# Recurrence steps threaded into the second output chunk, residual copies on two engines, and the second biases split earlier, in a two-layer kernel on one Trainium2 core

## The reference, cut to what matters

```
x = x + ffn0(cond0(x, cond))      # ffn0: gate/up products, quantised to 16 bits, sigmoid, down product
x = x + ffn1(cond1(x, cond))      # cond1: a recurrence over 128 steps; ffn1: 8 experts, top 2

cond1:  xw = x @ Wx + b
        h_t = tanh(xw_t + h_(t-1) @ Wh)          # 16 rows of 128, t = 0..127
ffn1:   logits = h @ router.T; top 2, softmax
        y = sum over the 2 of  gate * (gelu(h @ w1[e].T + b1[e]) @ w2[e].T + b2[e])
```

## Time and profile before

| | |
|---|---|
| Time, median of 3 runs | 302.99 us |
| Span of the profiled execution | 301.2 us |
| TensorE busy | 264.4 us, 88% |
| VectorE busy | 258.8 us, 86% |
| ScalarE busy | 215.6 us, 72% |
| GpSimd busy | 76.2 us, 25% |
| Mean granted TensorE clock | 0.947 |

### The profile page before, as it was taken

One profiled execution on the slowest core, in us unless ns is written; L12 is line 12 of the kernel. 1 busy time (PEld: TensorE's weight loads), 2 busy tenths in 40 slices (PEclk: granted clock), 3 DMA queues, 4 the chain that ended last, 5 costly groups with the idle time before them and its releaser, 6 DMA issues.

```text
span 301.2 us, 8834 instructions
## 1 busy us (share of the span) xinstructions
PE 264.4 (88%) x2716; PEld 205.5 (68%) x2716; DVE 258.8 (86%) x635; ACT 215.6 (72%) x455; POOL 76.2 (25%) x148
## 2 busy tenths in 40 slices
PE   4969940049989999999999999999999999999994
PEld 4824440016956777778888788888777887888874
DVE  4888999989898897779988799887799988889885
ACT  6367899998842677767777676667566766689892
POOL 3367997000025413011302112212110311101000
PEclk9989976557999999999999999999999999999999
DMA  6990443101500000000000000000001000001000
GB/s 186 314 310 4 84 94 76 28 0 35 90 17 2 0 3 1 0 2 2 19 0 0 2 3 26 2 0 0 1 2 30 8 0 0 2 1 37 0 2 27
DMA packets 24031, 10.63 MB, mean 35 GB/s; under 512 B 13355, under 2 KB 22982, under 8 KB 24006
## 3 DMA queue, kind: packets, MB, share of 16 engines
q1 hardware_dynamic: 23470, 10.05, 13.6%
q10 hardware_dynamic: 536, 0.26, 0.3%
HBM read 6.11 MB, written 1.05 MB: 24 GB/s over the span
## 4 chain that ended last, share of the span: by engine, by line
PE 79%; DVE 16%; issue 1%; ACT 1%; DMA 1%; SPq 0%; DVEq 0%
PE bank L893 78%; DVE peak L706 3%; DVE big L728 3%; DVE peak L633 2%; DVE big L711 1%; DVE big L744 1%; PE bank L937 1%; DMA y_sb<-in_cond 1%; PE bank L1017 0%; DVE big L746 0%; DVE wyT L779 0%; DVE pkm L626 0%; DVE big L738 0%; DVE x_sb L759 0%; DVE q L700 0%
## 5 line engine op out<-in xcount | busy, mean ns | idle before, releaser
L893 PE MATMUL bank<-big,wt 128*128 128x384 f16 (+2 forms) x480 | 124.8, 336 | 0.6 <-DVE big L872 0.5
L893 PE MATMUL bank<-wt,big 128*128 (+1 forms) x1536 | 111.5, 219 | 0.1
L872 DVE TENSOR_TENSOR big<-big 128x384 f16<-128x384 f32 (+2 forms) x160 | 93.2, 585 | 20.5 <-ACT big L594 16.1
L893 PEld LDWEIGHTS bank<-wt,big 128*128 128x128 f16 x1536 | 97.9, 97 | 16.2 <-issue 0.2
L592 ACT ACTIVATE big<-bank,miscT 128x384 f32<-128x384 f32 (+2 forms) x160 | 96.2, 602 | 15.3 <-PE bank L893 8.2
L893 PEld LDWEIGHTS bank<-q,wxh 128*128 128x128 f32 x254 | 44.4, 189 | 17.4 <-issue 3.4
L893 PEld LDWEIGHTS bank<-big,wt 128*128 (+1 forms) x480 | 50.0, 117 | 4.8 <-issue 1.1
L580 ACT ACTIVATE q<-bank (+1 forms) x112 | 20.6, 184 | 38.7 <-PE bank L893 37.9
L404 POOL CAST big<-q 128x64 f16<-128x64 f32 x32 | 13.2, 413 | 129.0 <-ACT q L580 126.5
L868 DVE CAST big<-big 128x512 f16<-128x512 f32 (+2 forms) x104 | 38.6, 372 | 4.8 <-ACT big L592 3.9
L827 DVE SCALAR_TENSOR_TENSOR wyT<-bank,gates,wyT 128x128 f32<-128x128 f32 x128 | 39.8, 343 | 1.0 <-issue 0.6
(11 more groups left out here) (165 smaller groups left out, 320.0 us busy)
## 6 DMA issues: line engine op xcount, KB each, us to landing
wnat<-in_w SPq DMA_DIRECT2D x8, 512.0 KB, 7.7
x_sb<-in_x SPq DMA_DIRECT2D x4, 256.0 KB, 4.3
out_block<-wyT SPq DMA_DIRECT2D x15, 64.0 KB
wn<-in_w_gate ACTq DMA_DIRECT2D x1, 192.0 KB, 4.9
wn<-in_w_up SPq DMA_DIRECT2D x1, 192.0 KB, 5.6
wn<-in_w_down SPq DMA_DIRECT2D x1, 192.0 KB, 5.7
b_in<-in_b SPq DMA_DIRECT2D x12, 4.0 KB
wt<-wyT SPq DMA_TRANSPOSE x8, 3.0
```

The source lines that it names most:

```text
L872: V.tensor_tensor(g_lo[:, par, f, 0:w], g32[:, f, 0:w], g_hi[:, par, f, 0:w], ALU.subtract).then_inc(g_lo_done, 1)
L893: return nc.tensor.matmul(o, l, r, start=start, stop=stop, skip_group_check=True)
```

## The change

It has four parts.

- The input part of the first 16 steps and step 0 go into chunk 1 of the down product, ahead of its ninth matmul (`PROJECT_AT = (1, 8)`), and into bank 7 and not bank 0. Steps 1 and 2 stand alone ahead of chunk 2, step 3 and the later ones every third matmul as before. One step is left behind chunk 4.
- The transposes of `x1` are divided: the first four, the last step, four more, then the input part of steps 16 to 39 (moved up from the head of the expert stage, and into bank 0 as before), then the last eight. The first transposes go to bank 4 and the second to bank 6. VectorE now copies the first two banks and ScalarE the last two (`ACC_SCALAR = (2, 3)`).
- VectorE adds the residual of chunk 3 before it splits chunk 2, splits chunk 3 behind its copies, and no longer splits chunk 4: GpSimd does (`split_x1` there). GpSimd also takes the low byte of chunk 2 from ScalarE (`LOW_SCALAR = 2`).
- `split_b2` stands ahead of the low bytes on GpSimd and waits for the fourth maximum (`pk_part` 4).

```diff
-LOW_SCALAR = 3
+LOW_SCALAR = 2
-ACC_SCALAR = 2
+ACC_SCALAR = (2, 3)
+X1_VECTOR = 4
+PROJECT_AT = (1, 8)
...
+        ps_first = banks[7]
-        ACC_BANKS = [6, 7, 1, 2]
+        ACC_BANKS = [4, 6, 1, 2]
...
@@ gpsimd
+            def split_b2():
+
+                pool.wait_ge(ld_b2, 16 * 3 * CTILES)
+                pool.wait_ge(pk_part, 4)
...
+            split_b2()
...
+            def split_x1(c):
+
+                at = slice(START[c], START[c + 1])
+                pool.wait_ge(x1_done, c + 1)
+                G.tensor_copy(x1_hi[:, at], x1[:, at]).then_inc(x1_hi_p, 1)
+                pool.wait_ge(x1_hi_p, c + 1 - X1_VECTOR)
+                G.tensor_tensor(x1_lo[:, at], x1[:, at], x1_hi[:, at], ALU.subtract).then_inc(x1_lo_p, 1)
+
             done = FIRST_STEPS // 4
             for i in range(done):
                 split_states(i)
-            split_b2()
+            split_x1(CH - 1)
@@ scalar
-            for k in range(ACC_SCALAR):
+            for k in ACC_SCALAR:
@@ vector
             make_x1(CH - 3)
+            make_x1(CH - 2)
             split_x1(CH - 3)
-            make_x1(CH - 2)
             make_x1(CH - 1)
-            split_x1(CH - 2)
             dve.wait_ge(wt_t[1], 16 * (W_CHUNKS - W_POOL))
-            for k in range(ACC_SCALAR, NK):
+            for k in range(ACC_SCALAR[0]):
                 dve.wait_ge(x1T_mm, k + 1)
...
-            split_x1(CH - 1)
-            dve.wait_ge(acc_s, ACC_SCALAR)
+            split_x1(CH - 2)
+            dve.wait_ge(acc_s, len(ACC_SCALAR))
@@ tensor
-                pe.wait_ge(x1_done, k + 2)
+                pe.wait_ge(x1_done, k + 2 if k else DOWN_BANKS.index(ACC_BANKS[0]) + 1)
...
-            step = 1
+            step = 0
             for c in range(CH):
                 if c == 2:
-                    pe.wait_ge(w_lo_s, W_CHUNKS - W_POOL)
-                    pe.wait_ge(small_w, 2)
-                    pe.wait_ge(bh_ready, 1)
-                    pe.wait_ge(x1_lo_done, 1)
-                    input_part(0, FIRST_STEPS)
-                    first_step(0)
+                    first_step(1)
+                    first_step(2)
+                    step = 3
...
+                        if (c, NJ * p + j) == PROJECT_AT:
+                            pe.wait_ge(small_w, 2)
+                            pe.wait_ge(bh_ready, 1)
+                            pe.wait_ge(x1_lo_done, 1)
+                            input_part(0, FIRST_STEPS, ps_first)
+                            first_step(0)
...
+            transpose_x1(0)
             for r in range(step, FIRST_STEPS):
                 first_step(r)
-            for k in range(NK):
-                transpose_x1(k)
+            transpose_x1(1)
+            pe.wait_ge(w_lo_s, W_CHUNKS - W_POOL)
+            pe.wait_ge(x1_lo_done, 2)
+            input_part(FIRST_STEPS, RNN_FROM[1])
+            transpose_x1(2)
+            transpose_x1(3)
...
-                    if c == 0 and first and s in (2, 3):
-                        pe.wait_ge(acc_s, s - 1)
+                    if c == 0 and first and s in (0, 2):
+                        pe.wait_ge(added, 1 + s // 2)
                     if c == 0 and first and s == NF:
-                        pe.wait_ge(added, 1)
+                        pe.wait_ge(acc_s, len(ACC_SCALAR))
...
-            pe.wait_ge(x1_lo_done, 2)
-            input_part(FIRST_STEPS, RNN_FROM[1])
```

More of the change, by code:

```diff
@@ L161, in program @@
             "gu_mm gu_sb gateq upq sig_done sig_round sig_16 g2_done g2q p_done oq o_hi_done o_lo_done o_lo_p")
-        down_mm, x1_done, x1_hi_done, x1_lo_done, x1T_mm = sems("down_mm x1_done x1_hi_done x1_lo_done x1T_mm")
+        down_mm, x1_done, x1_hi_done, x1_lo_done, x1_hi_p, x1_lo_p, x1T_mm = sems(
+            "down_mm x1_done x1_hi_done x1_lo_done x1_hi_p x1_lo_p x1T_mm")
         nat_done, small_w, rw_done = sems("nat_done small_w rw_done")
@@ L388, in _ @@
             split_weights(0, W_POOL)
+            def split_b2():
+                pool.wait_ge(ld_b2, 16 * 3 * CTILES)
+                pool.wait_ge(pk_part, 4)
+                link(G.tensor_scalar(b2_in[:, :], b2_in[:, :], WS, 0.0, ALU.mult, ALU.add))
+                link(G.tensor_scalar(b2_diag[:, :], b2_in[:, :], 1.0, 0.0, ALU.mult, ALU.add))
+                low = slice(2 * B2_ROWS, 3 * B2_ROWS)
+                G.tensor_tensor(b2_diag[low, :], b2_in[low, :], b2_diag[low, :], ALU.subtract).then_inc(b2_ready, 1)
+                pool.wait_ge(b2_ready, 1)
+            split_b2()
             def low_byte(c):
@@ L406, in split_states @@
                 G.tensor_tensor(h_lo[:, at], h32[:, at], h_hi[:, at], ALU.subtract).then_inc(h_lo_done, 1)
-            def split_b2():
-                pool.wait_ge(ld_b2, 16 * 3 * CTILES)
-                link(G.tensor_scalar(b2_in[:, :], b2_in[:, :], WS, 0.0, ALU.mult, ALU.add))
-                link(G.tensor_scalar(b2_diag[:, :], b2_in[:, :], 1.0, 0.0, ALU.mult, ALU.add))
-                low = slice(2 * B2_ROWS, 3 * B2_ROWS)
-                G.tensor_tensor(b2_diag[low, :], b2_in[low, :], b2_diag[low, :], ALU.subtract).then_inc(b2_ready, 1)
-                pool.wait_ge(b2_ready, 1)
             def split_gates(c):
@@ L993, in _, with input_part @@
             pe.wait_ge(xT_sb, NK)
-            def input_part(first, to):
+            def input_part(first, to, bank=ps_rnn):
                 at = slice(B * first, B * to)
-                o = ps_rnn[:, 0:B * (to - first)]
+                o = bank[:, 0:B * (to - first)]
                 mm(o, bh_rows[:, :], ones[:, 0:B * (to - first)], True)
@@ L1104, in pair @@
                         pe.wait_ge(h32_done, RNN_FROM[c])
-                        pe.wait_ge(x1_lo_done, CH)
+                        pe.wait_ge(x1_lo_done, X1_VECTOR)
+                        pe.wait_ge(x1_lo_p, CH - X1_VECTOR)
                         input_part(RNN_FROM[c], RNN_FROM[c + 1])
```

6 lines of the change are left out of this document (3 added, 3 removed).

## The result

| kernel | median us | runs | ratio to before | 95% interval |
|---|---|---|---|---|
| before | 302.99 | 5 (302.33 to 303.01) | 1 | |
| after | 300.31 | 5 (300.07 to 301.55) | 0.9933 | 0.9910 to 0.9957 |

2.7 us faster by the medians, where 301.9 (1.1 us) had been forecast; the low end of the range, 301.3, was too high as well. The ratio follows the means (302.77 and 300.73 us) and not the medians: by it the same ten runs give 2.0 us. The profiled execution of after has a span of 298.5 us, against 301.2.

A forecast was written before the change was run, and what follows sets the result against it. The chain of waits was read as 78% TensorE's matmul helper, the rest nearly all VectorE ahead of 82 us. Terms -1.14 - 0.3 + 0.3 + 0 gave -1.1 us, thus 301.9 us, range 301.3 to 302.9.

The forecast's parts named there:

- the four rivals: VectorE keeps the ports, 0.10; VectorE is late, 0.14; clock rises later, 0.07; steps not brought forward, 0.05.
- Steps 0 to 15: TensorE's recurrence steps threaded into the chunks: first slot of the last stage at 100.0 to 100.1, not 101.18, -1.14 us.
- Residual copies and first slots: VectorE's work ahead of slot 0's cast: TensorE's stall at the fifth slot shrinks from 0.47 to about 0.1, -0.3 us.
- Second biases at the fourth maximum: GpSimd's bias instructions moved to 61 us hold up VectorE's scaling by 0.4 to 0.5 us; cost taken as +0.3.
- Everything else ahead of the fifth spread: No stated term; the rest between profiled span (301.2 us) and median (302.99 us) was taken as unchanged.
- Third low byte: GpSimd's cast at 86.45 makes VectorE 1.18 us late through two chunks; cost 0, covered by 0.3 us at the tightest.
- Sum: All terms over the whole kernel: -1.1 us, span 300.1 us, time 301.9 us.

The follow-up runs named there:

- before_biases_moved: The kernel before with one edit, the second biases split at the fourth maximum, all else in the old order: ratio 1.0005 to before.
- biases_in_maxima: The changed kernel with the three second-bias instructions started one each with three products after the first one behind the fourth maximum: 301.06 us, ratio 0.9944.
- before_again: The kernel before, unchanged, measured once more: 302.78 us, ratio 0.9997.
- after_again: The changed kernel, unchanged, measured once more: 301.04 us, ratio 0.9945 to before.
- before_fill: The kernel before with 6 instead of 2 filling float32 matmuls in TensorE's wait ahead of the gate product: 302.63 us, ratio 0.9995.
- after_fill: The changed kernel with 6 instead of 2 filling float32 matmuls in TensorE's wait ahead of the gate product: 300.89 us, ratio 0.9943 to before.
- biases_late: The changed kernel with the second biases split behind GpSimd's own residual split of the last chunk: 302.74 us, ratio 1.0003 to before.
- low_byte_scalar: The changed kernel with the third low byte cast back on ScalarE: 303.28 us, ratio 1.0029 to before.
- biases_old_place: The changed kernel with the second biases back behind the fourth pair of states, ahead of the last chunk's residual halves: 301.72 us, ratio 0.9977 to before.

## Why the prediction was wrong

- *Direction and mechanism held.* The time is below before because the last stage starts earlier and its first slots don't wait; none of the four rivals came. The clock row doesn't rise later, TensorE doesn't wait in the third chunk, GpSimd's pending instruction gets the ports when VectorE's ends.
- *Steps 0 to 15, -1.14 us:* measured -1.35. Step 0 was forecast at 86.10 and came at 86.23, step 3 at 88.33 and came at 88.25, the transposes 97.13 and 97.05, and from there to the slot 2.78 us and not 2.88. Every mark up to there was right within 0.13 us; the term was 0.2 too small.
- *Residual copies and first slots, -0.3:* the stall is gone whole (-0.47), since VectorE was 0.23 us ahead of the GELU and not 0.05 behind. The term reaches -0.27 at the fifth slot and -0.17 one slot on, where the steps' own waits take some back. What the sum missed is whose this term was: without the biases' move the same threading has 0.97 us of waits there. The two places at which I added it up are one mechanism.
- *Second biases at the fourth maximum, +0.3:* **this is the step that failed.** The 0.5 us on VectorE was right to 0.05 us (1.26 measured, 1.2 forecast). Its way to TensorE wasn't: I took VectorE for the only bound up to the fifth maximum, and the weight chunks for starting when the fill ends, with an end of the range at 0. They start when ScalarE has cast the first two upper halves, 9.10 us behind its table load, in 14 of 15 traces, that of before among them. There was a gap of 0.24 us between the two ways in that execution and up to 1.0 in others. So the price is 0.3 in the kind of execution that I had (shown by before_biases_moved, and by biases_in_maxima, where it is saved) and 0 in the two others (shown by before_again against after_again, 19.9 us from the fourth maximum to the spread in both, and by before_fill against after_fill, 19.0 in both). That the 0.3 fits the first kind is luck: it is 0.5 less the gap, and I had it from the fill and the clock.
- *Everything else ahead of the fifth spread, 0:* a term that the sum took as nothing without a word (the span of one execution less the parts), **the other step that failed**, and the larger miss in the compared traces. The spread was due at 79.90 us and came at 78.43: 1.5 of the 1.6 us by which the span (298.5, forecast 300.1) was missed. after's trace is of a kind in which VectorE loses less to GpSimd between 40 and 50 us, and the range of the prediction had no room for that.
- *Third low byte, 0:* held. The fifth chunk is at 94.41 in before's time without a wait, its high part ready at 94.25: 0.16 us of cover, where 0.32 was forecast.
- *Sum.* -1.35 - 0.27 + 0.1 (given back in the slots) and 0 for the biases is -1.5 at the sixth slot, -1.5 to -1.8 at the end by the three pairs of traces, and -1.7 us by the times (0.9945 and 0.9943). The forecast was 0.6 short of that. The remaining 1.0 us of the first comparison is the draw: medians of five runs, in a kernel whose executions lie up to 2.5 us apart. Why the clock dips before 24 us in one place, in another or not at all stays open.

## What to carry to other kernels

Before a term is priced on one engine, ask which second chain ends close behind it, and by how much: take the difference between the two chains' arrival in the profiled execution, and if the start of the profile holds a dip of the clock, allow for it to be larger in other executions. When one part of a change brings work forward and another clears the place to which it comes, price them together, since here each alone gave 0.5 us in its trace and both together 1.7. For the total, a difference of one trace pair is to be counted from a mark behind the last unchanged code. Where the profile shows a pair of instructions that hold each other up and start 0.02 us apart, as in the earlier trace rows, expect the other order in other executions.

## What the runs showed of the hardware

- Short waits of TensorE can be followed by a fall of the granted clock to its lower level: in biases_late behind 1.44 us of waiting at 102.06 (lower level from 102.5 to 105.9), and in low_byte_scalar behind 0.94 and 0.27 us at 87.98 and 88.64 (lower level from 90.4 to 93.8, so 1.7 us after the second wait had ended). Waits of 0.57 and 0.40 us in biases_old_place had no fall behind them (granted 1.00 in all windows from 100 to 110 us). In low_byte_scalar the fall cost more than the waits: some 1.7 us, an estimate, half of its 3.4 us, against 1.2.
- The same program has the lower level before 24 us in different places from execution to execution, and its fourth maximum between 59.1 and 61.2 us.
- Which of VectorE and GpSimd is held up turns on less than half a microsecond: VectorE's scaling of 128x1024 took 1.68 us where it began 0.02 us behind GpSimd's tensor-tensor (before), and 0.86 where it came ahead (before_again); GpSimd's took 1.16 and 2.00 us.
